# Attention with fourth-power weights: one group of sums placed a step sooner in TensorE's order, and two fourth powers exchanged between engines

## What is computed

```python
s = jnp.einsum('bhtd,bhsd->bhts', q, k)
s = s - s.mean(axis=-1, keepdims=True)
mad = jnp.abs(s).mean(axis=-1, keepdims=True) + 1e-06
s = s / mad * score_gain
s = jnp.where(causal[None, None], s, jnp.asarray(-1000.0, s.dtype))
r = jnp.maximum(s, 0.0) ** POWER          # POWER = 4
att = r / (r.sum(axis=-1, keepdims=True) + 1e-06)
y = jnp.einsum('bhts,bhsd->bhtd', att, v)
```

## Time and profile before

| | |
|---|---|
| time before, median of 3 runs | 461.02 us (460.01 to 461.24) |
| the profiled execution's own time | 461.15 us |
| its span, first to last instruction | 458.8 us |
| PE, DVE, ACT, POOL busy, share of the span | 89%, 82%, 74%, 65% |

### The profile page before, as it was taken

How to read it: one execution, slowest core, us unless ns; L and a number is a source line. 1 busy time by engine, 2 the same in 40 slices (tenths; PEclk the granted TensorE clock), 3 DMA queues, 4 the chain that set the end, 5 groups by cost and what they waited for, 6 DMA issues and landing times.

```text
span 458.8 us, 13515 instructions
## 1 busy us (share of the span) xinstructions
PE 410.0 (89%) x5040; PEld 189.8 (41%) x5040; DVE 374.9 (82%) x927; ACT 340.1 (74%) x608; POOL 296.9 (65%) x217
## 2 busy tenths in 40 slices
PE   2998889886899999999998998999999869999895
PEld 1333335442444444444544444444444444534342
DVE  5666665649899999999999999999999975846543
ACT  3652246759899999999999999999999633463321
POOL 4002952529999999999999999999999930020000
PEclk9999999989999999999999999999999987999999
DMA  8000000354505124042051061150013000000001
GB/s 201 12 0 1 0 1 24 96 123 139 106 13 95 25 47 83 4 73 57 3 99 31 3 104 26 28 85 19 3 27 75 30 11 0 1 1 23 23 1 46
DMA packets 18238, 19.96 MB, mean 44 GB/s; under 512 B 4904, under 2 KB 10632, under 8 KB 18184
## 3 DMA queue, kind: packets, MB, share of 16 engines
q1 hardware_dynamic: 17896, 19.18, 20.0%
q10 hardware_dynamic: 288, 0.01, 0.0%
HBM read 13.02 MB, written 6.03 MB: 42 GB/s over the span
## 4 chain that ended last, share of the span: by engine, by line
PE 40%; ACT 18%; DVE 12%; issue 10%; POOL 4%; ACTq 1%; DVEq 0%
PE bank L1205 14%; PE bank L1242 10%; ACT bank L1346 8%; ACT arena L1365 6%; PE bank L1627 3%; PE bank L1593 3%; PE bank L1597 3%; DVE arena L1315 3%; POOL arena L1393 2%; DVE bank L1321 1%; PE bank L759 1%; PE bank L479 1%; POOL arena L530 1%; POOL arena L524 1%; DVE arena L1865 1%
## 5 line engine op out<-in xcount | busy, mean ns | idle before, releaser
L1393 POOL TENSOR_TENSOR arena<-arena 128x1024 f32<-128x1024 f32 (+1 forms) x144 | 240.8, 1708 | 10.0 <-ACT arena L1365 9.4
L1315 DVE SCALAR_TENSOR_TENSOR arena<-bank,masks 128x512 f32<-128x512 f32 x288 | 179.8, 681 | 5.3 <-PE bank L1205 5.3
L1365 ACT ACTIVATE arena<-arena 128x1024 f32<-128x1024 f32 (+1 forms) x160 | 148.1, 959 | 1.9 <-DVE arena L1315 1.3
L1205 PE MATMUL bank<-Q,K 128*32 128x512 bf16 (+3 forms) x1536 | 96.1, 327 | 14.2 <-DVE bank L1321 7.3
L1205 PE MATMUL bank<-K,Q 128*32 128x512 bf16 (+3 forms) x1536 | 92.5, 326 | 0.3 <-DVE arena L544 0.3
L1346 ACT ACTIVATE bank<-bank 128x1024 f32<-128x1024 f32 (+5 forms) x144 | 90.1, 625 | 0.4
L1321 DVE TENSOR_SCALAR_CACHE_REDUCE bank<-bank 128x896 f32<-128x896 f32 (+4 forms) x112 | 84.0, 779 | 0.0
L1242 PE MATMUL bank<-arena,Vq 128*32 128x512 f32 (+3 forms) x768 | 77.1, 486 | 1.3 <-POOL arena L1393 1.3
L1205 PEld LDWEIGHTS bank<-Q,K 128*32 128x32 bf16 x1536 | 37.1, 96 | 81.5 <-issue 24.3
L1242 PE MATMUL bank<-arena,ones_rows 128*32 128x512 f32 (+3 forms) x640 | 59.4, 464 | 0.0
L1205 PEld LDWEIGHTS bank<-K,Q 128*32 128x32 bf16 x1536 | 39.8, 96 | 28.6 <-DVE arena L1315 6.3
(11 more groups left out here) (188 smaller groups left out, 480.7 us busy)
## 6 DMA issues: line engine op xcount, KB each, us to landing
Q<-q_parts SPq DMA_DIRECT2D x21, 192.0 KB
K<-k_parts SPq DMA_DIRECT2D x14, 128.0 KB
att<-arena SPq DMA_DIRECT2D x28, 64.0 KB, 1.6
q_parts<-arena SPq DMA_DIRECT2D x6, 256.0 KB, 2.9
k_parts<-arena SPq DMA_DIRECT2D x6, 256.0 KB, 2.9
K<-k_parts SPq DMA_DIRECT2D x7, 192.0 KB
K<-k_parts SPq DMA_DIRECT2D x18, 64.0 KB
X<-in_L_attn_x SPq DMA_DIRECT2D x4, 256.0 KB, 4.8
```

The source lines that it names most:

```text
L1205: last = nc.tensor.matmul(m.bank[j:j + 32, at + lo:at + hi], left[par][:, g, blk * P + j:blk * P + j + 32], right[par][:, g, s0:s0 + hi - ...
L1315: nc.vector.scalar_tensor_tensor(Y(r, g)[:, y0:y0 + SPAN], m.bank[:, at:at + SPAN], 0.0, mask, ALU.max, ALU.mult).then_inc(relu_done, 1)
L1365: nc.scalar.activation(z, Y(r, g)[:, tile_low(r) - off(r):T - off(r)], ACT.Square)\
L1393: nc.gpsimd.tensor_tensor(z, z, z, ALU.mult).then_inc(fourth_p, 1)
```

## The change

Two edits. In `plan`, the sums of relu 0 stand behind the fills of step (1,2), and no longer behind those of (1,3). In `square_by_gpsimd`, the steps whose fourth power ACT makes are the last head of rounds 1 and 4, and no longer of rounds 1 and 3: that of (3,3), 1024 columns wide, goes to POOL, and that of (4,3), 512 wide, to ACT.

```diff
 def square_by_gpsimd(r, g):
-    return not (g == G - 1 and r in (1, 3))
+    return not (g == G - 1 and r in (1, 4))
...
                 if r == 1:
-                    return [[], some(last, "power", 4), [], some([q], "relu", 0)]
+                    return [[], some(last, "power", 4), some([q], "relu", 0), []]
```

## The result

The changed kernel takes 471.49 us in the median (469.69 to 473.96), the kernel before, on the same chip, 460.90 (460.01 to 461.24): a ratio of 1.0236 (95% interval 1.0195 to 1.0278). It is slower by 10.6 us in the medians; the forecast was 8.6 us more, 469.6. Medians and ratios here leave out single executions in a slow state, such as one of 1593.61 us of `e5_first_quad`.

What follows compares the result with a forecast made beforehand. The bound was taken as a ring: DVE all the way round plus a small DVE-PE-DVE handoff in round 3. 8.5 + 0.1 + 0 = 8.6 us on the profiled 461.15 gave 469.75, stated as 469.6; range 465.0 to 472.6.

Steps and rivals of the forecast that it cites:

- The mechanism of the steady quads: Relu 0's sums wait for ACT's copy of acc and delay (1,3)'s fills, stalling DVE: 8.5 us over seven quads.
- The stall: DVE's idle time before (1,3) in each quad with a copy: 1.21 us, from 245.11 to 246.32.
- Nothing lost: First quad: no copy to wait for, (1,3) ready at 115.35 before DVE arrives at 115.73, so no cost.
- Rival (e): PE's longer idle time lowers its clock in every changed quad: 25 us more, 495 us; chance 0.02.
- The fourth powers are worth nothing: Exchange between POOL and ACT: POOL's free time covers its extra 0.81 us, ACT's relief brings the ring 0.
- the 0.1 us in the second quad: POOL's backlog from the first quad makes PE late in round 0; 0.1 us on the path, between 0 and 0.6.
- The gap of 0.66 us before round 4: POOL's wait for ACT's squares in each quad, expected to be gone as the wider multiplication falls into it.
- ACT's 0.4 us: ACT has 0.4 us a quad less to do, a gain that ends at the square of (1,1), waiting for DVE.
- (a): PE's gain on DVE removes the waits at (3,0) and (3,1), 0.30 us each: 4.3 us more, 465.3; chance 0.10.
- (b): ACT is the bound and its 0.41 us less a quad comes through in all eight: 457.8 us; chance 0.07.
- (c): Change doesn't reach the time: relu 0 starts 0.5 us sooner, DVE has room at (1,3); 461 us; chance 0.04.
- (d): POOL or ACT's new square is later, PE waits for power 3 each quad: 3.2 us more, 472.8; chance 0.03.

Runs made afterwards that it cites:

- e5_first_quad: Kernel before, with relu 0's sums moved behind (1,2) in the first quad alone: 462.51 us, 1.0036.
- e3_copy_sooner: The whole change, plus the copy of acc one step sooner in ACT's order, ahead of the square of (1,1): 462.38 us, 1.0024 against the kernel before.
- e7_dve_more: Kernel before, with one more DVE relu of 512 columns at (1,2) in all quads but the last, its output unread: 464.28 us, 1.0062.
- e1_relu: Kernel before, with only relu 0's sums moved behind (1,2), fourth powers as before: 471.35 us, 1.0195.
- e4_later_quads: The whole change except in the first quad, where relu 0's sums stay behind (1,3): 469.55 us, 1.0194 against the kernel before.
- e2_fourths: Kernel before, with only the two fourth powers exchanged, relu 0 as before: 461.21 us, 1.0001.
- e6_act_more: Kernel before, with the fourth power of (4,3) also on ACT and so one less on POOL: 467.07 us, 1.0134.

## Why the prediction came out as it did

**The mechanism of the steady quads holds, step by step.** The copy does come no sooner: it ends 4.05 us after DVE's (1,0) begins (246.80 to 250.85), before it was 4.06 (240.26 to 244.32). Relu 0 waits for it, and takes 1.50 us to the next fill, as worked out. `e3_copy_sooner` shows that the copy is the cause, `e7_dve_more` that a stall of DVE counts in full, and `e1_relu` that the other edit has no part in it.

**The stall was put 0.1 us too short.** Counted from DVE's (1,0), PE was to start at 4.12 us, and starts at 4.19; the fills were to begin at 5.62, and begin at 5.69; DVE was to go on at 6.06, and goes on at 6.16. The two handoffs taken from the earlier trace rows were 0.06 and 0.44 us, and are 0.14 (250.85 to 250.99) and 0.47 (252.49 to 252.96) here. So 1.31 us were lost and not 1.21, and the quad is 1.33 longer: over seven quads that is some 0.8 us more than forecast, and the last has 0.2 on top.

**"Nothing lost" in the first quad is the step that failed.** I asked there only whether DVE would find its scores in time, and it did: it starts (2,0) 0.07 us late. I took the wait for POOL at power 0 as the same, since POOL's order is the same up to there. Its end is the same (119.46 against 119.38), but PE comes to it sooner, the gap grows from 1.34 to 1.93 us, and the clock falls there. That costs 2.5 us in the profile of after and 1.7 in the times of `e5_first_quad`. The one run of after that took 469.69 us, as forecast, had a mean granted clock of 0.989, as much as the profile of `e4_later_quads`, which has no such fall; the other three had 0.977 to 0.981. So that run may lack the fall, which no trace of it shows. Of the 12.9 us of the profile 9.5 are the mechanism that was forecast (at 8.5); the other 3.4, the first quad and what lies behind the attention, stood in the sum at nothing.

Rival (e) named the clock and looked for its fall at the wrong place, the gap in each steady quad: there PE is idle for 1.33 us a quad, and the clock is 1.00 throughout. It also had only the stretch behind the attention, and not that at 98.2 us. The Trainium skill ("TensorE: Matmul & The Clock Gate", section "A second HAM failure mode: psum-queue depth-cycling") tells of short idle times between groups of matmuls that make the clock swing; the trace of after agrees at most in the first quad (0.50 for 6.8 us), and not in the seven others.

**The fourth powers are worth nothing**, as forecast, by `e2_fourths`: 1.0001, and the 0.1 us in the second quad. The gap of 0.66 us before round 4 went as said. ACT's 0.4 us didn't come through. (Added up as printed, 1.06 + 0.13 - 0.66, ACT's relief is 0.53 us; with the overlap of the next instruction taken off, which the text leaves out, it is about 0.4.)

**The rivals.** (a) falls: both waits of round 3 stand in after with 0.23 and 0.22 us, since they begin at a relu of DVE. (b) falls with `e2_fourths`, though `e6_act_more` shows it to be nearer than the 0.07 it was given: the margin is about 0.17 us a quad. (c) falls by the time. (d) falls: among the waits of the four steady quads PE has none for POOL.

## What to carry to other kernels

A group of instructions that is moved ahead in an in-order queue gains nothing if what it waits for doesn't move, and it takes what now stands behind it along: look up the end of the awaited instruction, add the group's own length, and compare that with when the reader of the next group would be ready. Here the awaited instruction was a copy of 0.58 us on another engine, and its place in that engine's order decides nine tenths of the loss of a steady quad. Where a move lets an engine come sooner to a wait that doesn't end sooner, the gap there grows, so look at TensorE's granted clock around it, also in the one iteration that differs from the rest.

## What was new about the hardware

TensorE's granted clock fell from 1.00 to 0.50 around one gap in the first quad in all four profiled kernels whose gap was 1.84 to 1.98 us, and in none of the nine with 0.58 to 1.41 us, with PE as busy in the 14.7 us before in after as in the kernel before (10.31 and 10.23 us). In two of the four it fell 1.1 to 1.3 us into the gap, so the gap's full length is not what decided it. And 1.33 us of idle time in every quad of 33.29 us never lowered it. The stretch at half speed was 3.4 us long in `e5_first_quad` and 6.8 in after, for gaps of 1.96 and 1.93 us.

A release from ACT reached the waiting PE in 0.14 us here, where one from DVE had taken 0.06; and DVE began 0.47 us after the first matmul of a half, where I had 0.44 from another place.
